# Rotary turn of q in the last stage: its sine part's halves swapped by on-chip transfers and added on GpSimd

## The chip, the core and the metric

The kernel runs on one core of a Trainium2 chip. A core has five engines with their own instruction queues: TensorE (PE; PEld is its weight load), VectorE (DVE), ScalarE (ACT), GpSimd (POOL) and SyncE (SP, which here only issues transfers), 16 DMA engines, an on-chip memory of 128 partitions and the accumulator memory PSUM (8 banks of 128 x 512 words), which TensorE writes. Each queue runs in the order in which it was written; a semaphore wait at its head holds all that stands behind it. The metric is the device time of one execution in microseconds.

## The reference, cut to what matters

Input x is 32 sequences of 64 tokens with 128 features, with a context of the same shape. Four layers follow each other: an attention layer with quantised weights, an encoder-decoder style block (self attention, cross attention, feed-forward), a gated fusion with a pooled vision feature, and the last layer, which the change touches: RMS norm of x and of the context, grouped-query attention with 16 query heads of 64 features over 4 key heads, rotary position embedding on q and k, softmax, values, output projection, and a gated feed-forward layer. Its rotary embedding, and the scores, are

```python
def _rotate_half(x):
    x1, x2 = jnp.split(x, 2, axis=-1)
    return jnp.concatenate([-x2, x1], axis=-1)

def _apply_rope(x, cos, sin):
    return x * cos[None, None] + _rotate_half(x) * sin[None, None]
# scores = rope(q) @ rope(k).T / sqrt(64), q of 16 heads, k of 4, softmax over the 64 keys of a sequence
```

## The kernel before

The last layer works on eight groups g of four sequences (256 tokens), in rounds r. The features of a head lie on 64 partitions, two heads side by side (j = 0, 1), and the tokens in the free dimension.

How it turns q and k. Because a half swap of q can be moved over to k, q itself is never turned in full: `read_q` (line 1460) reads a bank of projected q from PSUM and writes two products, q times cosine and q times sine (one VectorE instruction of 128 x 1024). On the other side `rotate_k` (line 1470) and `sum_k` (line 1799) make turned k (`kc`) and a copy of it with the halves of each head swapped (`kcs`), both transposed by TensorE ("kt" and "ks") and copied to `k3` by ScalarE. `scores3` (line 706) then adds, for each tile, the product of the cosine part with k and that of the sine part with swapped k: c = 0 and c = 1.

What sets the order. Every engine's program is written out by hand. On TensorE the tables `HALVES`, `OPENING` and `ENDING` name, for each half of a round, the uses of the PSUM banks in order; the uses take the eight banks in a ring (`RING3`), so each waits until the one eight uses before it has been read. A step of round r works on group r ("s0", "s1" scores, "t0", "t1" transposed probabilities, "pv" values, "out"), on r + 1 ("in", "q0" to "q3"), on r + 2 ("l_in", "l_text", "k", "l_gate", "kt", "ks", "v", "l_back": the end of the third layer and k and v of the fourth) or behind ("m_in", "mg", "mu", "md": the feed-forward layer of r - 1 and r - 2). Before round 0 stands a ramp that fills q0 to q3 of group 0. The other engines have functions `opening`, `first_half` and `second_half` with the steps in the same order.

Steps that the prediction names:

- Half a round of softmax on VectorE: `smax3` (largest score, subtraction), then `sum3` after ScalarE's exponential, then `probs3` on GpSimd (line 1793), then the transposes on TensorE (line 742).
- VectorE's `l2_norm` (line 1434) opens a first half. It needs `rstd2`, made by GpSimd's `l2_rstd` (a `rsqrt`, line 1667) from the statistics `l2_stats` at the end of the half before. Behind `l2_norm` on VectorE stand the reads of mg1 and mu1 (lines 1496 and 1500), which TensorE's "md" (line 663) waits for, and then `smax3`.
- GpSimd's `l2_affine` (lines 1732, 1734) follows `l2_norm`, and ScalarE's `sq3` (line 941) follows that. Behind `sq3` on ScalarE stand `evac_pv3` (line 1027), an exponential (line 1014) and the read of "l_in" (line 981), which TensorE's "l_text" (line 639) waits for.
- In the loop ahead of `opening` the last thing on GpSimd is a `rsqrt` for the feed-forward layer of group 7 (semaphore f_ve, set by `ffn_sum(7)` on VectorE, which stands there behind the reads of q0 to q3 of group 0).

SyncE loads the inputs and then waits, group by group, for the final result and stores it.

## Time and profile before

| | |
|---|---|
| Median of three runs | 500.35 us (499.17 to 500.43) |
| The profiled execution | 500.22 us, its span 498.3 us, granted TensorE clock 0.982 of full |
| TensorE / weight load / VectorE busy | 447.4 (90%) / 355.5 (71%) / 378.3 us (76%) |
| ScalarE / GpSimd busy | 299.4 (60%) / 274.5 us (55%) |
| Chain that ended last | TensorE 54%, VectorE 22%, issue 13%, GpSimd 6%, ScalarE 4%, DMA 1% |

The span is the time from the first instruction to the last on the core; the execution's time is 1.9 us more. The last stage runs from about 262 us to the end: the ramp and round 0 until 293 us, round 1 until 323 us, rounds 2 to 5 of 27.8 us each until 434 us, then rounds 6 and 7 and the tail, where the steps for later groups fall away. After the inputs are loaded the DMA engines are nearly idle.

### The profile page before, as it was taken

To read this page: it belongs to the slowest core of one execution; us is meant where nothing else is said; L and a number is where in the kernel's file an instruction comes from. 1 tells how busy PE (TensorE), PEld (TensorE's weight loads), DVE (VectorE), ACT (ScalarE), POOL (GpSimd) and SP (SyncE) were. 2 spreads that over 40 slices of the span, in tenths; PEclk is the share of its full clock that TensorE was granted. 3 is DMA by queue.
4 is the path that set the end of the run, shared out by engine and by line. 5 is a ranking of instruction groups with operands and counts; after the bars stand their busy time and mean duration, and the time that the engine had idled before them with its cause. 6 is when DMAs were issued, how large, how long until landed. Compare 5 with 4: busy or idle time off the path is not lost.

```text
span 498.3 us, 16947 instructions
## 1 busy us (share of the span) xinstructions
PE 447.4 (90%) x6872; PEld 355.5 (71%) x6872; DVE 378.3 (76%) x918; ACT 299.4 (60%) x725; POOL 274.5 (55%) x332
## 2 busy tenths in 40 slices
PE   4798899999999999999989767999999999999885
PEld 4466666666666677689877546888888888878674
DVE  6699877688988888967879756868687676867642
ACT  2377676768686876666855426565566556553531
POOL 6465887579867787965662435445353545431210
PEclk9799999999999999999989979999999999999999
DMA  8970000000000000000000000000000000000000
GB/s 282 223 254 3 2 3 3 2 3 3 1 4 3 1 4 2 3 1 2 2 0 3 1 1 2 3 12 3 12 3 8 6 3 12 1 13 3 14 1 21
DMA packets 12420, 11.54 MB, mean 23 GB/s; under 512 B 5176, under 2 KB 10296, under 8 KB 12344
## 3 DMA queue, kind: packets, MB, share of 16 engines
q1 hardware_dynamic: 11624, 9.01, 6.8%
q10 hardware_dynamic: 720, 1.45, 0.8%
q8 instruction: 55, 0.90, 0.8%
q14 instruction: 21, 0.17, 0.1%
HBM read 9.42 MB, written 1.05 MB: 21 GB/s over the span
## 4 chain that ended last, share of the span: by engine, by line
PE 54%; DVE 22%; issue 13%; POOL 6%; ACT 4%; DMA 1%; DVEq 0%; POOLq 0%; ACTq 0%
DVE negm L1247 8%; PE ps L733 5%; PE ps L617 5%; DVE blocks L1238 5%; PE ps L447 4%; PE ps L633 4%; PE ps L655 4%; PE ps L465 3%; PE ps L610 3%; PE ps L625 2%; PE ps L544 2%; PE ps L531 2%; PE ps L495 2%; PE ps L756 2%; PE ps L663 2%
## 5 line engine op out<-in xcount | busy, mean ns | idle before, releaser
L1247 DVE TENSOR_REDUCE negm<-ps 128x8 bf16<-128x512 f32 x96 | 59.6, 683 | 25.2 <-PE ps L447 25.0
L832 ACT ACTIVATE p<-ps 128x512 f32<-128x512 f32 x96 | 54.7, 595 | 28.0 <-PE ps L455 26.8
L838 ACT ACTIVATE shared<-ps 128x512 f32<-128x512 f32 x96 | 57.0, 601 | 21.8 <-PE ps L465 20.4
L1740 POOL TENSOR_TENSOR wide<-wide,cv 128x1024 f32<-128x1024 f32 x24 | 45.6, 1902 | 32.5 <-ACT wide L822 32.5
L1793 POOL TENSOR_TENSOR probs<-p,rc 128x512 f32<-128x512 f32 x32 | 33.4, 1058 | 46.1 <-DVE rc L1533 45.9
L465 PE MATMUL ps<-cst,p 128*128 128x128 f32 x384 | 58.5, 276 | 0.4 <-ACT shared L838 0.4
L1667 POOL TENSOR_TENSOR rstd<-veps,neghalf 128x2 f32<-128x2 f32 x40 | 29.8, 745 | 48.5 <-DVE veps L1283 30.0
L465 PEld LDWEIGHTS ps<-cst,p 128*128 128x128 f32 x384 | 44.2, 141 | 11.5 <-issue 9.4
L1027 ACT ACTIVATE late<-ps 128x512 f32<-128x512 f32 x32 | 17.5, 594 | 35.9 <-PE ps L756 35.9
L1522 DVE TENSOR_REDUCE mx<-ps 128x8 f32<-128x512 f32 x32 | 21.9, 685 | 16.9 <-PE ps L733 16.9
L617 PE MATMUL ps<-shared,wq 128*128 128x256 f32 x128 | 30.7, 384 | 3.5 <-ACT shared L975 3.4
L455 PE MATMUL ps<-negm,idb 128*128 128x512 bf16 x96 | 29.3, 383 | 4.8 <-DVE negm L1247 4.7
L633 PE MATMUL ps<-wo,late 128*128 128x128 f32 x256 | 31.3, 275 | 2.2 <-ACT late L1027 2.2
L633 PEld LDWEIGHTS ps<-wo,late 128*128 128x128 f32 x256 | 30.7, 192 | 3.4 <-issue 2.8
L655 PE MATMUL ps<-in_t,wg 128*128 128x256 f32 x128 | 30.0, 380 | 0.7 <-ACT in_t L977 0.7
L617 PEld LDWEIGHTS ps<-shared,wq 128*128 128x128 f32 x128 | 23.1, 190 | 7.9 <-issue 3.7
L1238 DVE TENSOR_TENSOR blocks<-ps,rv 64x128 f32<-64x128 f32 x96 | 27.5, 286 | 1.0
L479 PEld LDWEIGHTS ps<-shared,blocks 128*32 128x32 f32 x1536 | 22.5, 110 | 7.6 <-ACT shared L838 6.5
L447 PE MATMUL ps<-wide,blocks 32*64 32x256 f32 x768 | 27.7, 397 | 0.0
L479 PE MATMUL ps<-shared,blocks 128*32 128x64 f32 x1536 | 26.4, 220 | 0.9 <-ACT shared L838 0.5
L655 PEld LDWEIGHTS ps<-in_t,wg 128*128 128x128 f32 x128 | 23.6, 190 | 3.7 <-issue 0.9
L1020 ACT ACTIVATE probs_t<-ps 128x512 f32<-128x512 f32 x32 | 18.9, 595 | 8.2 <-PE ps L742 7.9
(204 smaller groups left out, 1155.8 us busy)
## 6 DMA issues: line engine op xcount, KB each, us to landing
late<-in_mask_l SPq DMA_DIRECT2D x2, 512.0 KB, 11.6
result<-x_all SPq DMA_DIRECT2D x8, 128.0 KB, 1.8
x_all<-in_x_tok SPq DMA_DIRECT2D x1, 768.0 KB, 6.9
wide<-in_ctx_t SPq DMA_DIRECT2D x1, 768.0 KB, 8.4
rv<-in_rv ACTq DMA_DIRECT2D x1, 768.0 KB, 8.0
wa<-in_wa SPq DMA_DIRECT2D x1, 512.0 KB, 8.9
w<-in_w SPq DMA_DIRECT2D x2, 256.0 KB, 7.3
wq<-in_wq SPq DMA_DIRECT2D x1, 512.0 KB, 7.2
```

The costliest lines, as they stand in the source:

```text
L447: ins = mm(ps[b2 * S:b2 * S + S, S_BANK[r], t * 256:t * 256 + 256], q_t[rows[r], w % 2, cols], r_op[rows[r], w % 2, :, cols], start=(ph == ...
L465: ins = nc.tensor.transpose(bank[:, c * 128:c * 128 + 128], p3[:, n % 3, c * 128:c * 128 + 128], ident)
L479: ins = mm(N[32 * c:32 * c + 32, (t * 2 + b2) * 128:(t * 2 + b2) * 128 + 128] .rearrange("p (h y q) -> p h y q", h=2, y=2)[:, :, x, :], v_ ...
L617: ins = mm(bank_of(f"q{i}", g)[:, j * GT:j * GT + GT], wq3[:, 2 * i + j, :], hn_t[:, g % 2, :], start=True, stop=True, skip_group_check=True)
L633: ins = mm(bank_of("out", n)[:, 0:128], a3_t[:, g % 2, i, u * 128:u * 128 + 128], wo3[:, i, :], start=(i == 0), stop=(i == 7), skip_group_ ...
L655: ins = mm(bank_of(("mg", "mu")[j] + str(i), g)[:, c * GT:c * GT + GT], wg3[:, j, f * 128:f * 128 + 128], hm_t[:, g % 2, :], start=True, s ...
L832: A_(p3[:, n % 3, :], ps[:, S_BANK[r], :], ACT.Exp, scale=SC8).then_inc(sm["act_exp"], 1)
L838: A_(pt[:, w % 2, r, :], pt_bank(RG * w + r), ACT.Copy).then_inc(sm["act_pt"], 1)
L1238: ins = V.tensor_tensor(dst.rearrange("p (t m) d -> p t m d", t=TG), src, bias.unsqueeze(1).to_broadcast([S, TG, NP, DH]), ALU.add)
L1247: V.tensor_reduce(negm[:, n % 4, :], ps[:, S_BANK[r], :].rearrange("p (a k) -> p a k", k=S), AX.X, ALU.max, negate=True).then_inc(sm["dve_ ...
L1740: P.tensor_tensor(r_op[:, w % 2, :, :], k_t[:, w % 2, :].unsqueeze(1).to_broadcast([128, 4, GT]), head_masks.unsqueeze(2).to_broadcast([12 ...
L1793: P.tensor_tensor(probs[:, t % 2, :].rearrange("p (a k) -> p a k", k=S), p3[:, t % 3, :].rearrange("p (a k) -> p a k", k=S), rc3[:, t % 3, ...
```

## The change

q is turned in full. `read_q` now makes two VectorE instructions of 128 x 512 from a bank of q: first the sine product into a small buffer `q_sin` (two slots, in the memory of `ctx_tok`), then the cosine product into `q3`. SyncE waits for each sine product and issues four transfers from on-chip memory to on-chip memory, each of 32 partitions x 512 words (64 KB), which swap the two halves of each head into `q_swap` (also two slots). GpSimd's new `turn_q` adds `q_swap` onto the cosine part in place and raises `q_rot`. `scores3` does one product for each tile in place of two and waits for `q_rot` in place of VectorE's reads. The swapped k goes: its two additions on GpSimd, the "ks" transposes on TensorE and their copy on ScalarE; `k3` is half as large. A sine product waits until the transfers two before it have landed, and a transfer waits until the addition two before it is done. SyncE's queue now holds the transfers of group g + 2 ahead of the store of group g.

```diff
-        k3 = wide[:, 4096:7168].rearrange("p (g c a k) -> p g c a k", g=KEPT, c=2, a=2)
+        k3 = wide[:, 4096:5632].rearrange("p (g a k) -> p g a k", g=KEPT, a=2)
...
-        q3 = [[t.rearrange("p (c m q) -> p c m q", c=2, m=4) for t in half]
-              for half in ((wide[:, 0:2048], ctx_tok[:, :, :].rearrange("p n d -> p (n d)")),
-                           (blocks[:, 1024:3072], q3x[:, :]))]
-        kcs = sb("kcs", [128, TG, NK3])
+        q3 = [t.rearrange("p (a m q) -> p a m q", a=2, m=4) for t in (wide[:, 0:2048], q3x[:, :])]
+        q_sin, q_swap = (ctx_tok[:, n:n + 8, :].rearrange("p (a m) d -> p a (m d)", a=2) for n in (0, 8))
...
              ("l_gate", 2), ("t0", 0), ("in", 1), ("t1", 0), ("q0", 1), ("q1", 1)),
-            (("s0", 0), ("s1", 0), ("pv0", -1), ("pv1", -1), ("m_in", -1), ("kt", 2), ("ks", 2), ("q2", 1), ("q3", 1),
+            (("s0", 0), ("s1", 0), ("pv0", -1), ("pv1", -1), ("m_in", -1), ("kt", 2), ("q2", 1), ("q3", 1),
              ("out", -1), ("v", 2), ("mg0", -1), ("mu0", -1), ("l_back", 2), ("t0", 0), ("mg1", -1), ("mu1", -1), ("t1", 0)),
         )
...
+
+        def q_rows(g, i):
+            m = 2 * (i % 2)
+            return q3[g % 2][:, i // 2, m:m + 2, :].rearrange("p m (b q) -> p (m b) q", q=S)
...
             o_v = out.rearrange("(n p) d -> p n d", p=128)
+            def swap_halves(g):
+                half = HD3 // 2
+                for n in range(4 * g, 4 * g + 4):
+                    eng.wait_ge(sm["q_sin"], n + 1)
+                    if n >= 2:
+                        eng.wait_ge(sm["q_rot"], n - 1)
+                    for i in range(4):
+                        to, of = half * i, half * (i ^ 1)
+                        eng.dma_start(q_swap[to:to + half, n % 2, :], q_sin[of:of + half, n % 2, :])\
+                           .then_inc(sm[f"q_swap{n % 2}"], 16)
+
+            swap_halves(0)
+            swap_halves(1)
             for g in range(NG):
+                if g + 2 < NG:
+                    swap_halves(g + 2)
                 eng.wait_ge(*released("md", g))
                 eng.dma_start(o_v[:, TG * g:TG * g + TG, :], x_all[:, TG * g:TG * g + TG, :])\
                    .then_inc(sm["st_out"], 16)
...
                 for a in range(2):
-                    if u == 0 and a == 0:
-                        pe.wait_ge(*released("q1", g))
-                        pe.wait_ge(*released("ks", g))
-                    if u == 0 and a == 1:
-                        pe.wait_ge(*released("q3", g))
-                    for c in range(2):
-                        for i in range(2):
-                            for b in range(2):
-                                cols = slice(((2 * a + i) * 2 + b) * S, ((2 * a + i) * 2 + b) * S + S)
-                                for h in range(2):
-                                    for j in range(2):
-                                        rows = slice(j * S, j * S + S)
-                                        ins = mm(banks[j][h * S:h * S + S, cols], q3[gs][a][rows, c, 2 * i + h, toks[b]],
-                                                 k3[rows, g % KEPT, c, a, toks[b]], start=False, stop=True, skip_group_check=True)
+                    if u == 0:
+                        if a == 0:
+                            pe.wait_ge(*released("kt", g))
+                        pe.wait_ge(sm["q_rot"], 4 * g + 2 * a + 2)
+                    for i in range(2):
+                        for b in range(2):
+                            cols = slice(((2 * a + i) * 2 + b) * S, ((2 * a + i) * 2 + b) * S + S)
+                            for h in range(2):
+                                for j in range(2):
+                                    rows = slice(j * S, j * S + S)
+                                    ins = mm(banks[j][h * S:h * S + S, cols], q3[gs][rows, a, 2 * i + h, toks[b]],
+                                             k3[rows, g % KEPT, a, toks[b]], start=False, stop=True, skip_group_check=True)
...
             def read_q(g, i):
+                n = 4 * g + i
+                cos, sin = (cst[:, C_ROPEQ + c * S:C_ROPEQ + c * S + S].unsqueeze(1).to_broadcast([128, 2 * GB, S])
+                            for c in range(2))
+                bank = bank_of(f"q{i}", g).rearrange("p (b q) -> p b q", q=S)
+                if n >= 2:
+                    dve.wait_ge(sm[f"q_swap{n % 2}"], 64 * (n // 2))
+                V.tensor_tensor(q_sin[:, n % 2, :].rearrange("p (b q) -> p b q", q=S), bank, sin, ALU.mult)\
+                    .then_inc(sm["q_sin"], 1)
                 if g >= 2 and i == 0:
                     dve.wait_ge(sm["s3"], TG * (g - 1))
-                tab = cst[:, C_ROPEQ:C_ROPEQ + 2 * S].rearrange("p (c q) -> p c q", c=2).unsqueeze(2)\
-                    .to_broadcast([128, 2, 2 * GB, S])
-                m = 2 * (i % 2)
-                return V.tensor_tensor(q3[g % 2][i // 2][:, :, m:m + 2, :].rearrange("p c m (b q) -> p c (m b) q", q=S),
-                                       bank_of(f"q{i}", g).rearrange("p (b q) -> p b q", q=S).unsqueeze(1)
-                                       .to_broadcast([128, 2, 2 * GB, S]), tab, ALU.mult)
+                return V.tensor_tensor(q_rows(g, i), bank, cos, ALU.mult)
...
+            def turn_q(g, i):
+                n = 4 * g + i
+                pool.wait_ge(sm[f"q_swap{n % 2}"], 64 * (n // 2 + 1))
+                pool.wait_ge(*released(f"q{i}", g))
+                P.tensor_tensor(q_rows(g, i), q_rows(g, i), q_swap[:, n % 2, :].rearrange("p (b q) -> p b q", q=S), ALU.add)\
+                    .then_inc(sm["q_rot"], 1)
+
             def sum_k(g):
                 pool.wait_ge(sm["d_kc"], g + 1)
-                if g >= 1:
...
-                half = HD3 // 2
...
-                for j in range(2):
-                    P.tensor_tensor(kcs.rearrange("p t (n d) -> p (t n) d", d=HD3)[:, :, j * half:j * half + half],
-                                    swapped(kc[:, :, :], j), swapped(ks, j), ALU.add).then_inc(sm["d_ks"], 1)
-                pool.wait_ge(sm["d_ks"], 2 * g + 2)
                 P.tensor_tensor(kc[:, :, :], kc[:, :, :], ks[:, :, :], ALU.add).then_inc(sm["d_kr"], 1)
...
             def opening():
+                for i in range(4):
+                    turn_q(0, i)
                 rms_power(1)
                 probs3(0)
                 probs3(1)
+                turn_q(1, 0)
+                turn_q(1, 1)
                 probs3(2)
                 probs3(3)
+                l2_logits(2)
+                turn_q(1, 2)
+                turn_q(1, 3)
+                l2_fuse(2)
                 sum_k(2)
-                l2_logits(2)
-                l2_fuse(2)
...
             def second_half(r):
+                if r + 1 < NG:
+                    turn_q(r + 1, 0)
+                    turn_q(r + 1, 1)
                 if r + 2 < NG:
                     l2_fuse(r + 2)
                 if r < NG:
                     probs3(4 * r + 2)
                     probs3(4 * r + 3)
+                if r + 1 < NG:
+                    turn_q(r + 1, 2)
+                    turn_q(r + 1, 3)
```

Beside this, "ks" is dropped from `OPENING`, `EARLY_A`, `BY_ACT`, `part_in`, `fill`, and from ScalarE's reads.

GpSimd, from the end of the loop ahead of `opening` through the opening (before). `kcs` is the swapped k, `kc` the turned k, `rstd` on line 1667 the `rsqrt` that waits for f_ve of group 7, `rs` the one of `rms_power(1)`, `gp` is `l2_logits`, `fus` `l2_fuse`.

```order
L1812 TENSOR_TENSOR kc<-kc,wa 128x512
L1667 TENSOR_TENSOR rstd<-veps,neghalf 128x2
L1667 TENSOR_TENSOR rs<-ms,neghalf 128x2
L1793 TENSOR_TENSOR probs<-p,rc 128x512 x4
L1809 TENSOR_TENSOR kcs<-kc,wa 128x8x32 x2
L1812 TENSOR_TENSOR kc<-kc,wa 128x512
L1820 TENSOR_TENSOR gp<-ex,gvr 128x256
L1823 TENSOR_TENSOR gp<-gp,o_t 128x256
L1830 TENSOR_TENSOR fus<-wvis,vpr 128x256
L1834 TENSOR_TENSOR fus<-fus,a_t 128x256
```

The same place in the changed kernel, where line 1819 is `sum_k`, 1678 `rsqrt`, 1814 `turn_q` and 1804 `probs3`:

```order
L1819 TENSOR_TENSOR kc<-kc,wa 128x512
L1678 TENSOR_TENSOR rstd<-veps,neghalf 128x2
L1814 TENSOR_TENSOR wide<-wide,ctx_tok 128x512 x4
L1678 TENSOR_TENSOR rs<-ms,neghalf 128x2
L1804 TENSOR_TENSOR probs<-p,rc 128x512 x2
L1814 TENSOR_TENSOR q3x<-q3x,ctx_tok 128x512 x2
L1804 TENSOR_TENSOR probs<-p,rc 128x512 x2
L1827 TENSOR_TENSOR gp<-ex,gvr 128x256
L1830 TENSOR_TENSOR gp<-gp,o_t 128x256
L1814 TENSOR_TENSOR q3x<-q3x,ctx_tok 128x512 x2
L1837 TENSOR_TENSOR fus<-wvis,vpr 128x256
L1841 TENSOR_TENSOR fus<-fus,a_t 128x256
```

The four additions of group 0 stand behind the `rsqrt` that waits for f_ve. Two of group 1 stand between the pairs of probabilities, two between `l2_logits` and `l2_fuse`, and the sum of k moves from ahead of these to behind them.

GpSimd, from the first half of round 1 over its second half to the start of round 2 (before): `l2_logits`, `l2_fuse`, the probabilities, then `l2_rstd` (line 1667, waits for `l2_stats`) and `l2_affine` (lines 1732 and 1734).

```order
L1820 TENSOR_TENSOR gp<-ex,gvr 128x256
L1823 TENSOR_TENSOR gp<-gp,o_t 128x256
L1830 TENSOR_TENSOR fus<-wvis,vpr 128x256
L1834 TENSOR_TENSOR fus<-fus,a_t 128x256
L1793 TENSOR_TENSOR probs<-p,rc 128x512 x2
L1667 TENSOR_TENSOR rstd<-veps,neghalf 128x2
L1732 TENSOR_TENSOR wide<-wide,rv 128x256
L1734 TENSOR_TENSOR x_all<-wide,rv 128x256
```

The same in the changed kernel:

```order
L1827 TENSOR_TENSOR gp<-ex,gvr 128x256
L1830 TENSOR_TENSOR gp<-gp,o_t 128x256
L1814 TENSOR_TENSOR wide<-wide,ctx_tok 128x512 x2
L1837 TENSOR_TENSOR fus<-wvis,vpr 128x256
L1841 TENSOR_TENSOR fus<-fus,a_t 128x256
L1804 TENSOR_TENSOR probs<-p,rc 128x512 x2
L1814 TENSOR_TENSOR wide<-wide,ctx_tok 128x512 x2
L1678 TENSOR_TENSOR rstd<-veps,neghalf 128x2
L1743 TENSOR_TENSOR wide<-wide,rv 128x256
L1745 TENSOR_TENSOR x_all<-wide,rv 128x256
```

Two additions now stand ahead of `l2_fuse`, and two between the probabilities and `l2_rstd`.

## Rows read from the trace of the kernel before

**Rows 1.** Engines by stretch, round 4: us, busy of each engine, clock, DMA

```profile
378.50:406.31 27.81, 27.27 (x430) 23.29 (x429) 21.17 (x45) 16.98 (x47) 13.01 (x17) 1.00 0.03 7
```

**Rows 2.** TensorE timeline, round 3: start, us, engine, line, instruction

```profile
341.35 0.60 PE L610 MATMUL ps<-cst,kcs 128*128 128x128 f32 x4
...
351.56 1.16 PE L733 MATMUL ps<-wide,blocks 64*64 64x64 f32 x64
352.54 1.11 PE L733 MATMUL ps<-wide,q3x 64*64 64x64 f32 x64
353.47 1.04 PE L756 MATMUL ps<-probs_t,blocks 64*64 64x256 f32 x16
...
354.72 1.95 PE L663 MATMUL ps<-wd,wa 128*128 128x128 f32 x16
356.61 0.67 PE L639 MATMUL ps<-a_t,wl 128*128 128x256 f32 x2
...
360.60 0.65 PE L648 MATMUL ps<-tp_t,wl 128*128 128x256 f32 x2
```

**Rows 3.** VectorE timeline, same stretch

```profile
339.89 0.69 DVE L1522 TENSOR_REDUCE mx<-ps 128x8 f32<-128x512 f32 x1 [0.69 <-PE ps L733]
340.62 0.69 DVE L1524 TENSOR_TENSOR p<-ps,mx 128x512 f32<-128x512 f32 x1
341.23 0.68 DVE L1522 TENSOR_REDUCE mx<-ps 128x8 f32<-128x512 f32 x1
...
345.92 1.17 DVE L1466 TENSOR_TENSOR q3x<-ps,cst 128x1024 f32<-128x1024 f32 x1
...
351.05 0.60 DVE L1434 TENSOR_SCALAR wide<-wide,mv,rstd 128x128 f32<-128x128 f32 x2 [0.82 <-POOL rstd L1667]
...
352.35 0.69 DVE L1500 SCALAR_TENSOR_TENSOR wa<-w,ps 128x512 f32<-128x512 f32 x1
...
364.67 2.34 DVE L1466 TENSOR_TENSOR wide<-ps,cst 128x1024 f32<-128x1024 f32 x2
```

**Rows 4.** ScalarE timeline, same stretch

```profile
353.36 0.31 ACT L941 ACTIVATE sq<-x_all 128x128 f32<-128x128 f32 x1 [1.85 <-POOL x_all L1734]
...
354.59 1.08 ACT L1027 ACTIVATE late<-ps 128x512 f32<-128x512 f32 x2 [0.54 <-PE ps L756]
355.56 0.63 ACT L1014 ACTIVATE p<-p 128x512 f32<-128x512 f32 x1
356.08 0.39 ACT L981 ACTIVATE a_t<-ps 128x256 f32<-128x256 f32 x1
```

**Rows 5.** GpSimd timeline, same stretch

```profile
350.30 0.71 POOL L1667 TENSOR_TENSOR rstd<-veps,neghalf 128x2 f32<-128x2 f32 x1 [3.17 <-DVE veps L1283]
...
365.42 1.29 POOL L1812 TENSOR_TENSOR kc<-kc,wa 128x512 f32<-128x512 f32 x1
```

**Rows 6.** DMA issues: the page, and line 334's durations in ns

```profile
result<-x_all SPq DMA_DIRECT2D x8, 128.0 KB, 1.8
...
L334 SPq DMA_DIRECT2D mself<-in_mask_self x4: 312/342/809, 4.9 to 7.9; - x4
```

**Rows 7.** Timelines at the ramp: TensorE, VectorE, GpSimd

```profile
264.79 1.16 PE L733 MATMUL ps<-wide,ctx_tok 64*64 64x64 f32 x64 [0.28 <-DVE ctx_tok L1466]
...
260.12 2.36 DVE L1466 TENSOR_TENSOR wide<-ps,cst 128x1024 f32<-128x1024 f32 x2 [2.98 <-PE ps L617]
...
265.84 0.17 DVE L1283 TENSOR_SCALAR veps<-mv 128x2 f32<-128x2 f32 x1
...
266.09 0.74 POOL L1667 TENSOR_TENSOR rstd<-veps,neghalf 128x2 f32<-128x2 f32 x1 [6.12 <-DVE veps L1283]
```

**Rows 8.** Timelines at the start of round 1: TensorE, VectorE

```profile
290.91 0.66 PE L610 MATMUL ps<-cst,fus 128*128 128x128 f32 x2 [6.28 <-POOL fus L1834]
...
297.54 0.69 DVE L1522 TENSOR_REDUCE mx<-ps 128x8 f32<-128x512 f32 x1 [3.18 <-PE ps L733]
```

**Rows 9.** TensorE timeline, round 6

```profile
442.47 0.63 PE L742 MATMUL ps<-cst,probs 128*128 128x128 f32 x4 [0.78 <-POOL probs L1793]
```

More of the change, by code:

```diff
@@ L280, in build @@
         UNITS = (*PER_UNIT, "out")
-        BY_ACT = ("in", "l_in", "l_text", "l_gate", "l_back", "k", "kt", "ks", "v", "m_in")
+        BY_ACT = ("in", "l_in", "l_text", "l_gate", "l_back", "k", "kt", "v", "m_in")
         def half(r, h):
@@ L595, in part_in @@
                     src = [hm[:, g % 2, i, :] for i in range(TG)]
-                elif what in ("kt", "ks"):
-                    if what == "kt":
-                        pe.wait_ge(sm["d_kr"], g + 1)
-                    else:
-                        pe.wait_ge(sm["d_ks"], 2 * g + 2)
-                    src = [(kc if what == "kt" else kcs)[:, i, a * 128:a * 128 + 128] for a in range(2) for i in range(TG)]
+                elif what == "kt":
+                    pe.wait_ge(sm["d_kr"], g + 1)
+                    src = [kc[:, i, a * 128:a * 128 + 128] for a in range(2) for i in range(TG)]
                 elif what == "l_in":
@@ L687, in fill @@
                 take_bank(what, g)
-                if what in ("in", "m_in", "kt", "ks", "l_in", "l_back"):
+                if what in ("in", "m_in", "kt", "l_in", "l_back"):
                     ins = part_in(what, g)
@@ L991, in read @@
                     ins = A_(fused[:, gs, :], bank[:, 0:GT], ACT.Copy)
[L992 removed]
+                elif what == "kt":
                     if g >= KEPT:
                         act.wait_ge(sm["s3"], TG * (g - KEPT + 1))
[L995 removed]
+                    ins = A_(k3[:, g % KEPT, :, :].rearrange("p a k -> p (a k)"), bank, ACT.Copy)
                 else:
@@ L1032, in opening @@
                 read("kt", 1)
-                read("ks", 1)
                 sq3(1)
@@ L1054, in opening @@
                 read("kt", 2)
-                read("ks", 2)
             def first_half(r):
@@ L1111, in second_half @@
                 if r + 2 < NG:
-                    read("ks", r + 2)
                     read("v", r + 2)
@@ L1140, in _ @@
             read("kt", 0)
-            read("ks", 0)
             f_in(6)
```

9 lines of the change are left out of this document (2 added, 7 removed), and 4 rows, old and new, of the table OPENING.

## The prediction

> **What bounds the kernel now.** I read the stretches first. A steady round lasts 27.8 us, and TensorE is busy for all but 0.54 us of it at the full clock, while VectorE has 21.2 and GpSimd 13.0 us of work [rows 1]. So in rounds 2 to 5 TensorE sets the pace, and work taken from it counts until another chain is late. Then I read each engine's timeline of one round for the slack of those chains, and last the ramp and the start of round 1, where TensorE waits for VectorE and GpSimd [rows 7, 8].
>
> **What goes from TensorE.** The 128 score products of a half round run from 351.56 to 353.47: 0.98 us for the first 64 and 0.93 for the rest [rows 2]. Half of them go, 0.95 us for each half round and 15.3 us over 16. The "ks" transposes end 0.43 us after they start (the 0.60 in the row holds their pipelined end) [rows 2]: 8 x 0.43 = 3.4. If TensorE stayed the bound, a steady round would fall by 2 x 0.95 + 0.43 = 2.3 us to 25.5, and the whole by up to 18.7.
>
> **What comes.** VectorE: a bank of q costs one instruction of 1.17 us [rows 3]; a 512-wide one from PSUM takes 0.69, and its successor starts 0.61 after it [rows 3]. Two take 1.22 in place of about 1.1: +0.13 a bank, 0.5 a round. GpSimd: two additions of 0.71 each go (their 512-wide sister takes 1.29), four in-place additions of 128 x 512 come, at 1.28 each by that sister `kc` [rows 5]: some +3.7 us on 13.0 of 27.8, no bound by sum. ScalarE loses a copy. The ring of banks has 32 uses a round in place of 33; by the slack of the readers eight uses back I find none late, and cost it at nothing (its cover is 1 us or more on each; were one late, a few tenths a round).
>
> **The transfer, which the trace does not show.** Let D be the time from the end of a sine product until GpSimd can start its addition. SyncE issues four transfers one after the other. Issues of 32 partitions take 0.31 to 0.34 us [rows 6], so with a gap of 0.05 (my estimate) the fourth starts 3 x 0.39 = 1.2 us late. A store of 128 KB in rows of 512 B lands 1.8 us after its issue [rows 6]. Half the bytes in a quarter as many rows, and not to HBM: I take 1.6, plus 0.05 for the wake-up. D = 2.85. Bounds: 3 x 0.31 + 1.2 = 2.2 (each landing a third faster than the store) and 3 x 0.5 + 2.3 = 3.8. D is near the store's row, so I stay close to it.
> The Trainium skill (DMA: Bandwidth & Descriptors, Anatomy of one DMA) fits 2.0 us plus bytes over 436 GB/s to a transfer, 2.15 us for 64 KB, though for those that GpSimd issues, and its rules for kernel authors call transfers of this size mostly overhead. By the same fit the 128 KB store would take 2.3 us, where the row shows 1.8: the trace is faster. With 2.15 as the landing D would be 3.4 and the result that of the slow rival below.
>
> **A steady round, followed through the queues.** I anchor at N, the start of VectorE's `l2_norm` (351.05) [rows 3].
> - ScalarE's `sq3` starts at N + 2.31 [rows 4]. Its squares take 0.65, the two evacuations of values 0.97, the exponential 0.52 and the read of "l_in" 0.39 (starts and the last duration in rows 4); with 0.1 to wake TensorE, "l_text" can start at N + 4.95. Before, the evacuations started on TensorE's word at 354.59 and "l_text" at 356.61 = N + 5.56, so this chain had 0.6 us of slack.
> - From "l_text" to the first read of q on VectorE (364.67) are 8.06 us [rows 2, 3], through "l_gate" (360.60) and work that does not change.
> - Four reads of 0.61: 2.44. VectorE is then later than the shortened scores and sets the start of `smax3` in the second half: S = N + 15.45.
> - From `smax3` (339.89) to the read of q3 (345.92) are 6.03 us [rows 3]; with 0.13 for q2's pair and 0.69 for q3's sine product it ends at S + 6.85.
> - Then D = 2.85, the addition 1.28 and `l2_rstd` 0.71, which now stands behind it on GpSimd [rows 5]: in all 4.85 to the next N.
> Sum: 4.95 + 8.06 + 2.44 + 6.85 + 4.85 = 27.15. So the round falls by 0.65, not by 2.3. What is late: `l2_rstd` had followed `l2_stats` directly (350.30, with GpSimd idle for 3.17 us before it [rows 5]), and VectorE's reads of mg1 and mu1 stand behind `l2_norm`, ending 1.99 us after N (352.35 + 0.69 [rows 3]); TensorE's "md" waits for them, then "l_text" for ScalarE. I expect both waits, about 1.5 to 2 us of idle TensorE a round. Without the transfers in it the same loop, from S to `l2_norm` by the feed-forward reads and `l2_stats` (about 10.7 after S; before it was 351.05 - 339.89 = 11.16), gives 26.1: even a free transfer leaves 26.1 and not 25.5.
>
> **The ramp.** Here nothing covers D. VectorE starts to read q0 at 260.12, and TensorE runs the second half of scores(0) at 264.79, when q3 is read [rows 7]. After:
> - The "ks" of group 0 saves 0.4 of TensorE before. q0's sine product ends at 260.4, q1's at 261.6. The slots are two, so q2's waits for the first transfers (263.2) and q3's for the second, which queue behind them on SyncE (264.7). q3's cosine ends at 266.05.
> - `ffn_sum(7)` stands behind it on VectorE and ends 1.4 us after it (before: q3 read at 264.7, `veps` done at 265.84 + 0.17 [rows 7]): 267.45. GpSimd's `rsqrt`, 0.74 [rows 7], stands ahead of all additions: 268.25.
> - Additions 1 and 2 end at 269.5 and 270.75. q2's transfer had to wait for the first of them: it is there at 272.35, q3's 1.5 us of issues later, at 273.9. The fourth addition ends at 275.15.
> Scores(0) end near 275.9 with the second half at the lower clock, in place of 265.95: +10.0. TensorE has been idle most of the time from 263 to 275; after 6.28 us of idleness at 290.91 its rows of 128 x 128 show the lower clock (0.66 for two, where four take 0.60 in rows 2), so I expect it at 1.2 GHz for some microseconds here too; that eats what the shorter scores(1) give.
> Later in round 0 the q2 and q3 additions of group 1 stand ahead of `l2_fuse`, which TensorE's "l_back" waits for at 290.91 [rows 8]: sine of q3 ends at 296.4, addition at 300.8, fuse at 302.2: +11.3. The scores of round 1 then run half at the lower clock, and halving them gives 1.4 there. `smax3`, before at 297.54 [rows 8]: +9.9.
>
> **The sum** (lateness against before). Start of round 1 +9.9. Its second half: one score set less, 0.95, but S is set by VectorE's reads, +9.35; the transfer before N against 11.16 before: +0.5, so +9.9 at N of round 2. Four steady rounds at -0.65: +7.3. In round 6 probabilities set the pace (442.47 waits for GpSimd [rows 9]); measured from N they come 0.8 earlier, since `smax3` no longer waits for TensorE: +6.5. Scores of the second half of round 6, and of both halves of round 7, all on the path: -0.95 each, of which the last `q_rot` (turned q3 of group 7) takes back 0.4: +4.0. From there the chain is unchanged. Against the profiled execution, 500.22 us (span 498.3 and 1.9 around it): 504.2. The median of the runs, 500.35, is as good as the same. Forecast 504.
>
> D stands in the path nine times (twice in the ramp, once at the fuse, once into round 2, four rounds, once in round 7), so an error of 0.3 in D moves the result by 2.7 us.
>
> **Rivals.**
> - Faster: the transfers are hidden. If D is 1.9 or less (the four issues overlap and the landing is near 1.2), steady rounds go to 26.2, -1.6 each, and the ramp costs 8: 504.2 - 9 x 0.95 = 495.6. For it: SyncE has nothing else to do, and the DMA engines are nearly idle (share 0.03 [rows 1]). Against: one store alone takes 1.8 us [rows 6], and four issues stand in one queue. It decides for faster below D = 2.3 (504.2 - 9 x 0.55 = 499.2).
> - TensorE stays the bound everywhere and the ramp's cost is all there is: 500.2 + 10 - 18.7 = 491.5. For it: 0.54 us of idleness a round before. Against: the loop of 26.1 without any transfer.
> - No difference: the ramp costs some 4 us less, because work that I count as waiting moves under it (scores(1) at full clock, VectorE already free for `smax3`): about 500.
> - Slow transfers: landing 2.1 to 2.4 us as small ones sharing 16 engines. D = 3.4 to 3.6: 509 to 511. Then the additions q0 and q1 hold `l2_fuse` and the probabilities too.
>
> **How the numbers follow.** Forecast case 0.50, slow transfers 0.15, no difference 0.13, hidden transfers 0.17, TensorE-bound 0.05. A measurement of this kernel tells 0.3% (1.5 us) from no change. Slower by more: 0.45 of the forecast case and 0.15 of the slow one, 0.60. Within: 0.05 of the forecast case and 0.08 of the no-difference one, 0.13. Faster: the rest, 0.27. The forecast case alone spans 500 to 508 (D from 2.4 to 3.3); with the others the range is 494 to 510.
>
> **What would show it.** In the trace after: four issues of some 0.39 us apart and the last landing 1.6 us after its issue (a D of 2.3 or of 3.4 decides for a rival); scores(0) ending 10 us later, with GpSimd's four additions behind its `rsqrt`; steady rounds of 27.1 us with TensorE idle before "md" and "l_text"; GpSimd's `l2_rstd` right behind an addition; 0.95 us of scores a half round, where TensorE is at full clock. Rounds of 25.5 us, or scores(0) by 270, would show the forecast wrong; so would additions longer than 1.3 us.

## The result and the profile after

The changed kernel takes 529.52 us (median of 4 runs, 527.91 to 530.64) where the kernel before took 500.3 beside it (499.17 to 500.43): ratio 1.0604 [1.0579, 1.063], 29.2 us more. The forecast was 504.0, its range ended at 510.

From the page of the changed kernel: its engines, TensorE's clock in 40 slices, the chain that ended last, its costliest GpSimd addition and the transfers (in KB and us from issue to landing):

```profile
span 527.5 us, 15069 instructions
...
PE 442.1 (84%) x5816; PEld 343.2 (65%) x5816; DVE 385.7 (73%) x950; ACT 294.9 (56%) x717; POOL 302.3 (57%) x348
...
PEclk9999999999999999999857769999998999989999
...
PE 33%; DVE 24%; issue 20%; POOL 13%; ACT 5%; SPq 3%; DMA 2%; DVEq 0%; POOLq 0%; ACTq 0%
...
L1814 POOL TENSOR_TENSOR q3x<-q3x,ctx_tok 128x512 f32<-128x512 f32 x16 | 20.3, 1267 | 35.0 <-DMA ctx_tok<-ctx_tok 35.0
...
ctx_tok<-ctx_tok SPq DMA_DIRECT2D x128, 64.0 KB, 2.0
```

Over the whole span no engine is the bound: the busiest has 84% (before, TensorE had 90%), and GpSimd waits 35.0 us for transfers before additions of q that go to `q3x` (19.9 more before those to `wide`). The same as [rows 1], stretches of the changed kernel (us, busy of each engine, clock, share of the DMA engines): the ramp, round 0 to the first `l2_norm`, and two steady rounds, from one `l2_norm` to the next:

```profile
262.50:285.00 22.50, 7.73 (x138) 5.64 (x142) 10.40 (x23) 3.90 (x12) 7.52 (x8) 0.54 0.15 36
285.00:313.13 28.13, 16.95 (x110) 13.14 (x100) 18.99 (x39) 8.78 (x23) 13.27 (x13) 0.79 0.16 38
...
343.77:374.10 30.33, 26.46 (x344) 21.59 (x340) 22.61 (x50) 16.36 (x46) 16.50 (x18) 1.00 0.16 40
374.10:403.82 29.72, 25.05 (x230) 20.41 (x223) 21.76 (x50) 15.77 (x45) 16.45 (x18) 0.94 0.17 41
```

The four steady rounds last 30.33, 29.72, 31.37 and 29.52 us (mean 30.24) where they were 27.8 [rows 1] and 27.15 was forecast. In the ramp TensorE works 7.7 of 22.5 us, and the mean granted clock is 0.54 of full, so mostly the lower level of 1.2 GHz.

GpSimd of the changed kernel in a steady round and at the ramp; L1814 is the addition of a swapped sine part, L1837 and L1841 `l2_fuse`, L1678 a reciprocal root:

```profile
267.89 0.74 POOL L1678 TENSOR_TENSOR rstd<-veps,neghalf 128x2 f32<-128x2 f32 x1 [11.54 <-DVE veps L1291]
268.61 2.52 POOL L1814 TENSOR_TENSOR wide<-wide,ctx_tok 128x512 f32<-128x512 f32 x2
274.64 1.26 POOL L1814 TENSOR_TENSOR wide<-wide,ctx_tok 128x512 f32<-128x512 f32 x1 [3.51 <-DMA ctx_tok<-ctx_tok]
277.08 1.26 POOL L1814 TENSOR_TENSOR wide<-wide,ctx_tok 128x512 f32<-128x512 f32 x1 [1.19 <-DMA ctx_tok<-ctx_tok]
...
293.43 1.27 POOL L1814 TENSOR_TENSOR q3x<-q3x,ctx_tok 128x512 f32<-128x512 f32 x1 [7.40 <-DMA ctx_tok<-ctx_tok]
...
361.87 1.27 POOL L1814 TENSOR_TENSOR q3x<-q3x,ctx_tok 128x512 f32<-128x512 f32 x1 [3.02 <-DMA ctx_tok<-ctx_tok]
364.39 1.27 POOL L1814 TENSOR_TENSOR q3x<-q3x,ctx_tok 128x512 f32<-128x512 f32 x1 [1.25 <-DMA ctx_tok<-ctx_tok]
365.62 0.61 POOL L1837 TENSOR_TENSOR fus<-wvis,vpr 128x256 f32<-128x256 f32 x1
...
369.00 1.27 POOL L1814 TENSOR_TENSOR q3x<-q3x,ctx_tok 128x512 f32<-128x512 f32 x1
372.14 1.26 POOL L1814 TENSOR_TENSOR q3x<-q3x,ctx_tok 128x512 f32<-128x512 f32 x1 [1.87 <-DMA ctx_tok<-ctx_tok]
373.35 0.71 POOL L1678 TENSOR_TENSOR rstd<-veps,neghalf 128x2 f32<-128x2 f32 x1
```

In [rows 5] the root of the steady round followed `veps` after a wait; here it stands behind the addition of q3. The first addition of group 1 has waited 7.40 us.

VectorE of the changed kernel in the same round; L1475 is a sine product, L1533 the start of `smax3`, L1442 `l2_norm`, L1423 and L1429 small products of stage 2 that read two tiles of SBUF:

```profile
356.35 0.92 DVE L1423 TENSOR_TENSOR gvr<-exr,gv 128x4 f32<-128x4 f32 x1
...
357.27 0.68 DVE L1475 TENSOR_TENSOR ctx_tok<-ps,cst 128x512 f32<-128x512 f32 x1
...
359.66 0.68 DVE L1533 TENSOR_REDUCE mx<-ps 128x8 f32<-128x512 f32 x1
...
362.30 1.12 DVE L1429 SCALAR_TENSOR_TENSOR wvis<-gate,ex 128x256 f32<-128x256 f32 x1
...
366.17 0.65 DVE L1475 TENSOR_TENSOR ctx_tok<-ps,cst 128x512 f32<-128x512 f32 x1
...
369.65 0.63 DVE L1291 TENSOR_SCALAR veps<-mv 128x2 f32<-128x2 f32 x1
374.10 0.60 DVE L1442 TENSOR_SCALAR wide<-wide,mv,rstd 128x128 f32<-128x128 f32 x2 [3.81 <-POOL rstd L1678]
```

D is the time from the end of a sine product to the start of its addition, as in the prediction. Here it is 361.87 - 357.95 = 3.92 us for q0, and 372.14 - 366.82 = 5.32 for q3 (4.5 to 6.0 in the four rounds beside it). The 128 issues (ns, smallest, median, largest; then their landing in us):

```profile
L363 SPq DMA_DIRECT2D ctx_tok<-ctx_tok x128: 507/590/1882, 258.7 to 486.9; - x128
...
DMA to landing us min/median/max: 1.9/2.0/3.6
```

SyncE of the changed kernel in this round: q0's four issues, the last two of q2's and the first of q3's, and the long one, q3's third:

```profile
357.97 2.42 SPq L363 DMA_DIRECT2D ctx_tok<-ctx_tok  x4
...
366.04 1.22 SPq L363 DMA_DIRECT2D ctx_tok<-ctx_tok  x2
...
367.36 0.54 SPq L363 DMA_DIRECT2D ctx_tok<-ctx_tok  x1
...
368.57 1.47 SPq L363 DMA_DIRECT2D ctx_tok<-ctx_tok  x1
```

Four take 2.42: starts some 0.6 apart, where the forecast had 0.39. q3's sine product ends at 366.82, but q2's issues end at 367.26: 0.54 of queue (with the start), then gaps of 0.57, 0.64 and 1.50 to the fourth at 370.07, and 2.07 to the addition.

The third gap is not an ordinary one. The issues and landings of two sets of four, q0's in the next round and q0's in the one behind it (ns; landing in us):

```profile
L363 SPq DMA_DIRECT2D ctx_tok<-ctx_tok x4: 507/591/1882, 388.3 to 390.1; - x4
...
DMA to landing us min/median/max: 1.9/2.9/3.4
```

```profile
L363 SPq DMA_DIRECT2D ctx_tok<-ctx_tok x4: 507/591/592, 418.4 to 420.2; - x4
...
DMA to landing us min/median/max: 1.9/2.0/2.0
```

Where an issue is long, the transfers just ahead of it land late as well (up to 3.4 us in place of 2.0): I read both as one pause of about 1 us. Each of the five rounds from N = 313.13 to 464.71 has one, in a set of q0, q1 or q3, so this run does not show a round without it. Why it comes is open.

### The profile page after: what moved, and what is told of

The parts are those of the page before. It is cut to its first block, busy times and chain, and to the rows that moved or that the text cites. A ratio compares the mean times of both kernels' runs of the same rounds, so it can differ in the third digit from the quotient of the medians.

```text
span 527.5 us, 15069 instructions
## 1 busy us (share of the span) xinstructions
PE 442.1 (84%) x5816; PEld 343.2 (65%) x5816; DVE 385.7 (73%) x950; ACT 294.9 (56%) x717; POOL 302.3 (57%) x348
## 4 chain that ended last, share of the span: by engine, by line
PE 33%; DVE 24%; issue 20%; POOL 13%; ACT 5%; SPq 3%; DMA 2%; DVEq 0%; POOLq 0%; ACTq 0%
DVE negm L1255 7%; DVE blocks L1246 4%; PE ps L464 4%; PE ps L482 3%; SPq L363 3%; POOL wide L1814 2%; PE ps L548 2%; POOL probs L1804 2%; PE ps L647 2%; PE ps L512 2%; PE ps L639 2%; PE ps L561 2%; POOL q3x L1814 2%; PE ps L424 2%; PE ps L425 1%
## 5 line engine op out<-in xcount | busy, mean ns | idle before, releaser
L1255 DVE TENSOR_REDUCE negm<-ps 128x8 bf16<-128x512 f32 x96 | 59.6, 683 | 23.9 <-PE ps L464 23.7
L844 ACT ACTIVATE p<-ps 128x512 f32<-128x512 f32 x96 | 54.7, 595 | 27.8 <-PE ps L472 26.7
L1751 POOL TENSOR_TENSOR wide<-wide,cv 128x1024 f32<-128x1024 f32 x24 | 45.5, 1896 | 31.2 <-ACT wide L834 31.2
L1678 POOL TENSOR_TENSOR rstd<-veps,neghalf 128x2 f32<-128x2 f32 x40 | 29.7, 743 | 36.8 <-DVE veps L1291 18.3
L1814 POOL TENSOR_TENSOR q3x<-q3x,ctx_tok 128x512 f32<-128x512 f32 x16 | 20.3, 1267 | 35.0 <-DMA ctx_tok<-ctx_tok 35.0
L647 PE MATMUL ps<-wo,late 128*128 128x128 f32 x256 | 33.0, 284 | 2.2 <-ACT late L1039 2.2
L647 PEld LDWEIGHTS ps<-wo,late 128*128 128x128 f32 x256 | 32.4, 201 | 3.4 <-issue 2.8
L1533 DVE TENSOR_REDUCE mx<-ps 128x8 f32<-128x512 f32 x32 | 21.9, 684 | 16.9 <-PE ps L745 16.9
L669 PE MATMUL ps<-in_t,wg 128*128 128x256 f32 x128 | 32.9, 406 | 0.7 <-ACT in_t L989 0.7
L1814 POOL TENSOR_TENSOR wide<-wide,ctx_tok 128x512 f32<-128x512 f32 x16 | 20.1, 1268 | 21.1 <-DMA ctx_tok<-ctx_tok 19.9
L1039 ACT ACTIVATE late<-ps 128x512 f32<-128x512 f32 x32 | 17.4, 591 | 25.5 <-PE ps L768 25.5
L754 PE MATMUL ps<-cst,probs 128*128 128x128 f32 x128 | 20.8, 289 | 9.5 <-POOL probs L1804 9.5
L1475 DVE TENSOR_TENSOR ctx_tok<-ps,cst 128x512 f32<-128x512 f32 x32 | 21.5, 673 | 9.5 <-PE ps L631 5.8
```

The source lines that it names most:

```text
L647: ins = mm(bank_of("out", n)[:, 0:128], a3_t[:, g % 2, i, u * 128:u * 128 + 128], wo3[:, i, :], start=(i == 0), stop=(i == 7), skip_group_ ...
L669: ins = mm(bank_of(("mg", "mu")[j] + str(i), g)[:, c * GT:c * GT + GT], wg3[:, j, f * 128:f * 128 + 128], hm_t[:, g % 2, :], start=True, s ...
L844: A_(p3[:, n % 3, :], ps[:, S_BANK[r], :], ACT.Exp, scale=SC8).then_inc(sm["act_exp"], 1)
L1255: V.tensor_reduce(negm[:, n % 4, :], ps[:, S_BANK[r], :].rearrange("p (a k) -> p a k", k=S), AX.X, ALU.max, negate=True).then_inc(sm["dve_ ...
L1678: P.tensor_tensor(dst, src, neghalf[:, 0:n], ALU.pow).then_inc(done, 1)
L1751: P.tensor_tensor(r_op[:, w % 2, :, :], k_t[:, w % 2, :].unsqueeze(1).to_broadcast([128, 4, GT]), head_masks.unsqueeze(2).to_broadcast([12 ...
```

## The experiments

Each ran against the kernel before on the same chip, whose medians there were 498.45 to 498.9 us. Theory A says that the transfers' path (issues, landing, queue) makes the loss. N is the start of `l2_norm`; the distance from one N to the next is the round. The cuts of code are against the changed kernel, in the last experiment against the kernel before.

**Three kernels that take the edit apart.** The halved score products, without "ks", with VectorE's two instructions per bank, and with neither transfers nor additions:

```
-                        pe.wait_ge(sm["q_rot"], 4 * g + 2 * a + 2)
+                        pe.wait_ge(*released(f"q{2 * a + 1}", g))
 (swap_halves and the body of turn_q left out)
```

> Neither transfers nor additions: the scores wait for VectorE's cosine products, the sine products are made and used by nobody (the turn of q is left out). What the halved scores and the missing swapped k are worth alone. Theories A and B: rounds near 26 us (held by the loop through l_text, smax3 and l2_rstd, not by TensorE's 25.5), no loss in the ramp, 482 to 488 us; the distance to the kernel without transfers is what the additions cost, 5 to 12 us by A, 25 or more by B. Theory C: above 515 us.

Measured: 489.95 us, ratio 0.982 [0.9797, 0.9842]. The additions as well, of the sine part itself, its halves not swapped (four slots in place of two):

```
-                P.tensor_tensor(q_rows(g, i), q_rows(g, i), q_swap[:, n % 2, :]...
+                P.tensor_tensor(q_rows(g, i), q_rows(g, i), q_sin[:, n % 4, :]...
```

> The changed kernel without its transfers: GpSimd adds the sine product itself, with its halves not swapped (so q isn't turned rightly), four slots of sine products in place of two; the additions stay where they are. Theory A (the way of a bank of q from VectorE's sine product through four issues on SyncE and a landing is too long for the places where it has to be covered: the ramp, the group 1 additions, each round): the 5.3 us between q3's sine product and its addition go, steady rounds fall from 30.3 to 26 to 27 us, scores(0) end near 268 in place of 279, and the time is 490 to 500 us. Theory B (the additions themselves, four of 1.27 us a round in GpSimd's queue and beside VectorE, carry the loss): it stays above 515 us. Theory C (halved scores and the shorter ring of banks upset TensorE by themselves): above 520 us.

Measured: 497.12 us, ratio 0.9953 [0.9934, 0.9973]. And one transfer of 128 partitions for four of 32 (two slots again, halves not swapped):

```
-                    for i in range(4):
-                        to, of = half * i, half * (i ^ 1)
-                        eng.dma_start(q_swap[to:to + half, n % 2, :], q_sin[of:of + half, n % 2, :])...
+                    eng.dma_start(q_swap[:, n % 2, :], q_sin[:, n % 2, :]).then_inc(sm[f"q_swap{n % 2}"], 16)
```

> One transfer of 128 partitions in place of the four of 32, with the halves not swapped: as many bytes, a quarter of the issues. Theory A with the serial issues (0.63 us each on SyncE, 2.5 us a bank) as its larger part: sine product to addition 2.7 us in place of 3.9 to 5.3, steady rounds near 28 us, time 505 to 512 us. If the landing of small transfers or the bytes were what counts, it would stay at 525 to 530 us. Theories B and C: 525 to 530 us as well.

Measured: 505.2 us, ratio 1.0126 [1.0073, 1.018]. By the ratios, times 500: halved scores and no "ks" -9.0 us, the additions +6.7, one landing +8.6, three more issues per bank +23.9. The intervals of the four ratios do not overlap, so each step is clear of noise. Two steps hold more than their name: the third goes from four slots back to two as well, and slots alone were worth 5.6 us in the changed kernel (below); the last also replaces a transfer of 256 KB by four of 64.

Where each step costs is read from N. The first N of the four kernels stands at 291.62, 301.29, 303.63 and 313.13 (293.76 in the kernel before), and the mean of the four rounds from the second N on is 26.17, 26.30, 27.28 and 30.24 us. So the additions cost almost nothing in a steady round; they cost 9.7 us before the first N, and the total is 6.7. Even with no transfer the second half of scores(0) starts at 271.56, behind GpSimd's additions, which follow its root (265.82). The landing costs 1.0 a round, the three issues more 3.0 a round and 9.5 before the first N.

The steady round of the kernel with additions and no transfer, and of the one with one transfer per bank:

```profile
357.12:383.32 26.20, 24.89 (x292) 20.71 (x283) 21.47 (x49) 16.32 (x46) 16.53 (x18) 1.00 0.02 7
```

```profile
389.35:416.49 27.14, 25.22 (x307) 21.00 (x300) 22.41 (x50) 16.35 (x46) 16.60 (x18) 1.00 0.13 46
```

26.2 is near the loop that the forecast had without a transfer (26.1), and TensorE is not full in it (24.89 of 26.20; it waits 0.73 us ahead of "l_text" and 0.54 ahead of q0). The transfers, not GpSimd's work, make the difference to 30.2.

**The ramp's order.** GpSimd adds group 0 ahead of the reciprocal root of group 7:

```
+                if g == NG - 1:
+                    for i in range(4):
+                        turn_q(0, i)
                 pool.wait_ge(sm["f_ve"], g + 1)
 (and the same three lines no longer in opening)
```

> The changed kernel with one edit in GpSimd's order: the four additions of group 0 stand ahead of the rsqrt of group 7 (which waits for VectorE's ffn_sum(7)), not behind it. Theory A: the first two additions start at 262.7 and 265.3 in place of 268.6 and 269.9, scores(0) end 6 us earlier, and nothing later gives it back: 522 to 524 us. If the ramp's lateness were absorbed by waits later in round 0: 527 to 530 us.

Measured: 525.12 us, ratio 1.0527 [1.0482, 1.0572]: 4 us less. N of round 1 comes at 308.38 in place of 313.13. Round 1 then takes 33.05 us in place of 30.64 and gives half of that back, which theory A had denied; the next four have the same mean (30.25 and 30.24). The ramp's order is a part, not the cause.

**Two banks by one set of transfers.**

```
-                for n in range(4 * g, 4 * g + 4):
-                    eng.wait_ge(sm["q_sin"], n + 1)
+                for n in (2 * g, 2 * g + 1):
+                    eng.wait_ge(sm["q_sin"], 2 * n + 2)
...
-                        eng.dma_start(q_swap[to:to + half, n % 2, :], q_sin[of:of + half, n % 2, :])...
+                        eng.dma_start(q_swap[to:to + half, :, :], q_sin[of:of + half, :, :])...
```

> As the changed kernel, but one set of four transfers moves two banks (rows of 4 KB in place of 2 KB): 32 issues fewer on SyncE in the first two groups and half of all. Theory A (the time of a turned q3 is its own four issues of 0.63 us, a landing of 2.0, and q2's four issues ahead of it): q3's transfer no longer queues behind q2's, but both additions then stand behind the one landing, 3.9 + 2.6 = 6.5 us after q3's sine product where the changed kernel has 5.3 + 1.3 = 6.6. So the steady round stays at 30.1 to 30.3 us, the ramp gains about 0.5: 528 (525 to 531). Rival F: the time goes with the number of issues, whatever waits behind them (24 us for three more per bank between one and four transfers): half of the issues gives back about half, 517 to 519, rounds of 28.7.

Measured: 535.63 us, ratio 1.0752 [1.0713, 1.0792], slower than either theory said. Rival F falls: half the issues gave nothing back, since q3's own four and the landing stay. In this kernel's round from N = 345.53, GpSimd's additions of q2 and q3, and SyncE's four issues for them:

```profile
373.82 2.48 POOL L1814 TENSOR_TENSOR q3x<-q3x,ctx_tok 128x512 f32<-128x512 f32 x2 [2.84 <-DMA ctx_tok<-ctx_tok]
```

```profile
367.90 2.41 SPq L363 DMA_DIRECT2D ctx_tok<-ctx_tok  x4
...
DMA to landing us min/median/max: 2.2/2.3/4.0
```

From the end of the last issue (370.31) to the addition are 3.5 us; in the changed kernel, where the last begins at 370.07 and takes the median 0.59, they were 1.5. I read this as the pause again and not as the size of the transfer: in 13 of the 16 sets the fourth lands after the ordinary 2.3 us, in three after 3.6 to 4.0. The one round without a pause in its sets (N = 408.31 to 438.04) takes 29.73 us, a little less than theory A's 30.1 to 30.3; the other three take 31.2 to 31.5. That both additions stand behind one landing, so that each pause reaches the path, would explain the longer rounds, but it is argued from four rounds.

**Four slots.** `q_sin` takes all of `ctx_tok`, `q_swap` a free part of `shared`:

```
-                    if n >= 2:
-                        eng.wait_ge(sm["q_rot"], n - 1)
+                    if n >= 4:
+                        eng.wait_ge(sm["q_rot"], n - 3)
```

> As the changed kernel, but four slots for the sine parts and four for the swapped ones, so that no sine product and no transfer waits for a slot. Theory A: only the ramp changes. All 16 issues run through (10 us from 258.7), the last lands near 270.8, the second half of scores(0) starts near 272.3 in place of 278.4, steady rounds stay at 30.2: 523.5 (521 to 526). Rival I: slots also cost in steady rounds (q2's transfer waits for the addition of q0): rounds of 29.2, 517. Rival J: the ramp's lateness is absorbed later (TensorE at the lower clock anyway): 528 to 530.

Measured: 522.26 us, ratio 1.0491 [1.0439, 1.0542]. The mean of the four rounds from N = 338.11 to 459.13 is 30.26, as in the changed kernel (30.24): theory A's answer for the slots in steady rounds, and I and J fall. The second half of scores(0) starts at 272.62 in place of 278.40. N of round 1 comes 7.2 us earlier (305.91), of which round 1 (32.20 in place of 30.64) gives 1.6 back.

**The additions of q0 and q1 behind `l2_fuse` and the probabilities** (with four slots; in round 0 all four of group 1 stand behind them):

```
             def second_half(r):
-                if r + 1 < NG:
-                    turn_q(r + 1, 0)
-                    turn_q(r + 1, 1)
                 if r + 2 < NG:
                     l2_fuse(r + 2)
...
                     probs3(4 * r + 3)
                 if r + 1 < NG:
+                    turn_q(r + 1, 0)
+                    turn_q(r + 1, 1)
                     turn_q(r + 1, 2)
```

> As the kernel with four slots, and GpSimd adds q0 and q1 behind l2_fuse and the probabilities (in round 0 all four of group 1 stand behind them). Theory K (the additions of q0 and q1 cost by what stands behind them on GpSimd, and by slowing wvis of VectorE beside them, 1.12 us in place of 0.43): against four slots the steady round falls by 0.5 to 0.9 and round 0 by about 3: 516 (513 to 520). Rival L: these waits lie off the path, only q2 and q3 set it, and the additions now crowd in front of l2_rstd: 522 to 525.

Measured: 518.75 us, ratio 1.0427 [1.0375, 1.048]. The interval overlaps that of four slots, so the total alone does not settle it; the rounds do: mean 29.23 (N from 340.36 to 457.28), 1.0 less. The 3 us that theory K had for round 0 did not come: the first N is 0.8 earlier (305.12), and round 1 takes 35.24 us where it took 32.20. One term of the steady round is plain, `wvis` in the changed kernel and in this one (busy us, mean ns):

```profile
L1429 DVE SCALAR_TENSOR_TENSOR wvis<-gate,ex 128x256 f32<-128x256 f32 x8 | 5.4, 672 | 0.0
```

```profile
L1430 DVE SCALAR_TENSOR_TENSOR wvis<-gate,ex 128x256 f32<-128x256 f32 x8 | 3.3, 416 | 0.0
```

**`l2_rstd` ahead of q3's addition** (with all of the last; the addition is no longer in second_half):

```
                 if 1 <= r < NG - 1:
                     l2_rstd(r + 1)
+                if 2 <= r < NG:
+                    turn_q(r, 3)
+                if 1 <= r < NG - 1:
                     l2_affine(r + 1)
```

> As the kernel with four slots and the additions of q0 and q1 behind, and from the third group on GpSimd's addition of q3 stands behind l2_rstd instead of ahead of it. Theory M (in a steady round what q3's transfer holds is l2_rstd and so l2_norm, while the scores that need q3 are due some 2.7 us later): l2_norm starts 1.7 us earlier, l2_affine stands behind the addition and gives 1.2 back at most; the round falls from 29.2 to 27.6 to 28.2, and with four to six rounds of it 511 (508 to 514). Rival N: the scores' own wait for q3 takes its place at once and the round stays at 29 or more: 517 to 520.

Measured: 515.46 us, ratio 1.0326 [1.0277, 1.0375]; mean round 28.59 (N from 335.60 to 449.95), between the two theories. Beside the addition (421.64, 1.27 us) `l2_norm` takes 1.54 us, where it took 0.60:

```profile
421.71 1.54 DVE L1443 TENSOR_SCALAR wide<-wide,mv,rstd 128x128 f32<-128x128 f32 x2 [1.90 <-POOL rstd L1679]
```

**Half of the change, where a half round covers the transfer.** The kernel before, in which groups 2 to 7 turn q0 and q1 in full: VectorE's one instruction per bank stays, SyncE swaps the sine parts of both by four transfers into a free part of `shared`, GpSimd adds them where it was idle, and `ks` and the products with swapped k stay for q2 and q3 alone (groups 0 and 1 stay as they were):

```
+                for i in range(4):
+                    to, of = half * i, half * (i ^ 1)
+                    eng.dma_start(q_swap[to:to + half, :, :], q3[g % 2][0][of:of + half, 1, :, :])...
...
-                    for c in range(2):
+                    for c in range(1 if g >= 2 and a == 0 else 2):
...
                     probs3(4 * r + 2)
                     probs3(4 * r + 3)
+                if r + 1 < NG:
+                    turn_q(r + 1)
```

> The kernel before, with one part of the change: from the third group on only q0 and q1 are turned in full, by four transfers for both after q1's product is read, two additions on GpSimd in the 3.2 us in which it waited before l2_rstd, half the products of these heads and half the ks transposes. Groups 0 and 1, and q2 and q3 of all, stay as before. Theory G (a landing of some 3.9 us costs nothing where a half round lies between it and its reader): TensorE's round of 27.8 loses 0.95 of scores and 0.2 of transposes, 26.6 to 26.8, no ramp cost: 494 (492 to 497), ratio 0.987. Rival H: GpSimd's two additions end after 3.2 us and hold l2_rstd, or slow VectorE's reads of mg0 and mu0 beside them, so the round stays at 27.8 or more: 500 to 504.

Measured: 490.46 us (489.81 to 491.23), ratio 0.9843 [0.9806, 0.988]: faster than both kernels, and rival H falls. The interval lies clear of 1. Its steady round, and GpSimd in it:

```profile
346.57:373.22 26.65, 26.11 (x364) 22.14 (x362) 21.21 (x45) 16.74 (x48) 14.90 (x18) 1.00 0.11 27
```

```profile
341.83 1.04 POOL L1814 TENSOR_TENSOR probs<-p,rc 128x512 f32<-128x512 f32 x1 [0.52 <-DVE rc L1554]
342.83 2.51 POOL L1824 TENSOR_TENSOR blocks<-blocks,shared 128x512 f32<-128x512 f32 x2
345.83 0.71 POOL L1688 TENSOR_TENSOR rstd<-veps,neghalf 128x2 f32<-128x2 f32 x1 [0.49 <-DVE veps L1304]
```

The additions follow the probabilities without a wait (the landing is hidden) and end 0.49 us before the root starts on VectorE's `veps`. TensorE is the bound again, 26.11 of 26.65. The time is 3.5 us below the 494 that was expected and below its range (492 to 497); by the ratios, 0.984 for 0.987, it is 1.4 us.

## Why the prediction was wrong

The direction was right and the loop that the forecast followed is there; its size was not, and in three of five rounds another chain sets the pace. By its own steps:

- **What goes from TensorE:** right. Halved scores and no "ks" give 9.0 us, with steady rounds of 26.2 and not 25.5. That the loop of 26.1 without a transfer was met within 0.1 is in part luck: from "l_text" to the first read of q the kernel without transfers takes 8.61 (forecast 8.06), from `smax3` to the next N 10.31 (forecast about 10.7).
- **The step that failed is D,** forecast 2.85 with an upper bound of 3.8; it measured 3.92 for q0 and 5.32 for q3, the one in the loop. Three terms of it were short. The issue: starts about 0.63 apart, where 0.39 was taken (0.34 for a load of 32 partitions [rows 6] and 0.05 of gap), so 0.7 over three gaps, and the pause in q3's third issue took another 0.9. The kernel before gives only a hint of such pauses: one of the four loads in [rows 6] took 0.81, and of its eight stores the median lands after 1.8 us and one after 3.4. The landing: 2.07 with the wake-up where 1.65 was taken, below the 1.8 of the store [rows 6], on an argument (fewer bytes, fewer rows) that no row bore out: 0.4. And the queue: 0.5 behind q2's issues, since the forecast had four issues in 1.56 us and so no queue in the round. Together 2.5. The Trainium skill (DMA: Bandwidth & Descriptors, Anatomy of one DMA) gives 2.15 us for a transfer of 64 KB, which I set aside; measured is a landing of 2.0, so there the page was nearer than my value.
- **The round,** by the forecast's steps from N = 343.77: 4.90, then 8.60 to the first q read (forecast 8.06), 2.39 for the reads, 7.16 to q3's sine end (6.85), D 5.32 (2.85), 1.96 for addition and root: 30.33 in place of 27.15. D holds 2.5 of the 3.2 us. The other 0.85 are contention that the forecast did not weigh: `gvr` takes 0.92 beside GpSimd's addition of k, where it took 0.38 beside the shorter one of swapped k (+0.54), and `wvis` 1.12 beside the addition of q0, where it takes 0.42 in the kernel without transfers (+0.7). Of the 1.24, 0.4 do not show, because the stretch from `smax3` to q3's sine product was forecast too long: it takes 6.45 in that kernel and not 6.85.
- **"Additions q0 and q1 hold `l2_fuse` and the probabilities"** stood only in the rival of slow transfers. It happened: they run at 361.87 and 364.39, `l2_fuse` at 365.62 although VectorE's `wvis` ended at 363.42. In three of the five rounds this second chain sets the end of the round: there GpSimd adds q2 and q3 in one go behind the probabilities (340.58 and 2.49 us on, in the round before), without a wait for their transfers, and the root follows. It is late by the transfers of q0 and q1, whose additions stand 2.5 us apart by four issues. In the other two rounds q3's addition does wait, each time for a pause: the long issue above, and a landing of 3.6 us in the round that ends at 435.19 (D 6.0). Without the pause D of q3 would be 0.54 + 1.84 + 2.0 = 4.4 (an estimate from the queue, the gaps and the median landing). With the first two additions moved behind, the round falls by 1.0.
- **The ramp:** the queue of GpSimd was right (root, two additions, then two that wait for transfers), the time +13.6 and not +10.0: scores(0) end at 279.53. The first two additions start 0.4 us later than forecast, the third 2.3 (274.64, for 272.35) and the fourth 3.2 (277.08, for 273.9): from the freed slot to the third addition are 4.8 us, where D was 2.85. Both halves of the scores were slow (1.13 us for 32 products, 0.69 in a steady round), on a stretch whose mean clock is 0.54.
- **From the ramp to the first `l2_norm`:** +9.9 was forecast, +19.4 measured (313.13 against 293.76). The clock is 0.79 on that stretch, the first addition of group 1 waits 7.40 us, and the probabilities behind it come at 297.18. The kernels taken apart divide the 19.4: -2.1 with halved scores alone, +9.7 for the additions, +2.3 for the landing (with the slots), +9.5 for the three issues. How much of it is the clock was not run apart; four slots take back 7.2 (305.91), and with the order moved 8.0 (305.12).
- **The rest:** five rounds took back nothing but added 10.9 us (lateness +19.4 at N of round 1, +30.25 at that of round 6), where -2.6 was forecast (+9.9 to +7.3). In rounds 6 and 7 the lateness falls by 1.0 to 29.2, where -3.3 was forecast.
- **The sum and the range:** the forecast said that D stands in the path nine times. With its own sensitivity D of 5.3 gives 504 + 9 x 2.45 = 526, and D of 4.4, without the pauses, 518. That the first comes near the measured 529.5 is partly luck: three of five rounds do not wait for q3's transfer, and in the ramp D was 4.8. The bound of 3.8 rested on an issue of 0.5 and one bank by itself; neither a bank behind another bank's issues nor a pause was in it, nor the contention and the second chain.

## What to carry over

A transfer's cost on a critical path is its issues in their queue, with the issues of the transfer ahead, plus the landing; bound it for the last of a burst and not for one alone, and allow for a pause. Put such a transfer where a half round lies between it and its reader, which hides a pause too, and leave it out where it does not: this change for 12 of the 32 banks, so placed, gives 1.6%, for all of them it costs 6%. And count what a GpSimd addition does to VectorE's instructions beside it, not only its own time.
